# Moving one-time work across a joint, and reordering the queues of the steps behind it

## The reference

```python
x = _layernorm(x + L0(x))   # mixes x scaled by row sums of adj, by their squares, and a softmax's row sums, with one weight
x = _layernorm(x + L1(x))   # A_hat @ x, @ W1.T, batchnorm over all images, relu, @ W2.T, batchnorm
x = _layernorm(x + L2(x))   # two graph convolutions, then LSTMs over windows of 1, 2, 3, 4 nodes
x = _layernorm(x + L3(x))   # h = x @ fc.T + b, then 8 Euler steps:
#   h = h + (1/8) * (sigmoid(alpha)/2 * (adj @ h - h) + h @ w_eff - h + x0),  w_eff = (w * clip(d, 0, 1)) @ w.T
```

## Time and profile before

| | us |
|---|---|
| median of 3 runs | 982.8 (981.35 to 983.01) |
| the profiled execution, its own time | 981.68 |
| its span in the profile | 979.6 |
| TensorE busy | 915.4 (93%) |
| VectorE busy | 645.8 (66%) |
| ScalarE busy | 576.6 (59%) |
| GpSimd busy | 314.6 (32%) |

### The profile page before, as it was taken

The page is one execution under the profiler, slowest core; times in us unless marked ns, Lnnn a source line. Parts: engine busy times, 40 slices in busy tenths (PEclk is TensorE's granted clock), DMA queues, the critical chain, the costliest instruction groups (busy, mean ns, idle before and its releaser), DMA issues.

```text
span 979.6 us, 14819 instructions
## 1 busy us (share of the span) xinstructions
PE 915.4 (93%) x5115; PEld 792.3 (81%) x5115; DVE 645.8 (66%) x1576; ACT 576.6 (59%) x1292; POOL 314.6 (32%) x527
## 2 busy tenths in 40 slices
PE   8799998968899979999999999999999999999996
PEld 6688886346788658998998898899899889978986
DVE  5889995863467755666667666665766666675644
ACT  5467666823464556557737855774685576467352
POOL 2766555411101242035216304421620442150120
PEclk9999999989799989999999999999999999999999
DMA  5321201301011010101100110120011001000100
GB/s 177 119 75 57 74 33 46 122 27 65 0 33 55 1 33 1 54 2 44 56 11 11 33 66 1 44 65 1 12 33 66 1 22 44 1 12 1 33 22 22
DMA packets 26596, 38.56 MB, mean 39 GB/s; under 512 B 3333, under 2 KB 12422, under 8 KB 26010
## 3 DMA queue, kind: packets, MB, share of 16 engines
q1 hardware_dynamic: 26088, 36.05, 11.1%
q10 hardware_dynamic: 434, 1.57, 0.4%
HBM read 21.89 MB, written 15.73 MB: 38 GB/s over the span
## 4 chain that ended last, share of the span: by engine, by line
PE 55%; DVE 9%; POOL 7%; ACT 6%; issue 3%; ACTq 0%; POOLq 0%; DVEq 0%
PE psum L140 16%; PE psum L142 15%; PE psum L141 15%; PE psum L1811 2%; PE psum L1812 2%; PE psum L1815 2%; ACT gate L1378 1%; ACT x L1409 1%; POOL x_rstd L1311 1%; ACT raw L1474 1%; POOL out_rstd L1311 1%; POOL node_l L1329 1%; PE psum L1986 1%; DVE in_h L1543 1%; DVE shared L1617 1%
## 5 line engine op out<-in xcount | busy, mean ns | idle before, releaser
L1378 ACT ACTIVATE gate<-psum,gate_bias 128x256 f32<-128x256 f32 (+2 forms) x296 | 144.1, 559 | 85.2 <-PE psum L1815 62.4
L140 PE MATMUL psum<-in_h,wih_h 128*128 128x256 f32 (+2 forms) x312 | 107.3, 344 | 11.2 <-DVE in_l L1547 7.9
L142 PE MATMUL psum<-in_h,wih_l 128*128 128x256 f32 (+2 forms) x312 | 104.1, 334 | 0.0
L141 PE MATMUL psum<-in_l,wih_h 128*128 128x256 f32 (+2 forms) x312 | 103.6, 332 | 0.0
L1528 DVE TENSOR_TENSOR gate<-gate 128x256 f32<-128x256 f32 (+2 forms) x48 | 23.9, 499 | 88.9 <-ACT gate L1378 88.8
L140 PEld LDWEIGHTS psum<-in_h,wih_h 128*128 128x128 f32 x312 | 59.2, 190 | 22.9 <-DVE in_l L1547 11.6
L1345 POOL TENSOR_TENSOR gate<-in_h,in_l 128x512 f32<-128x512 f32 x14 | 17.9, 1303 | 164.7 <-DVE in_l L1547 164.7
L140 PE MATMUL psum<-e_h,shared 128*128 128x384 f32 x180 | 62.0, 345 | 5.5 <-DVE shared L1617 3.2
L1381 ACT ACTIVATE gate<-cell 128x512 f32<-128x512 f32 (+2 forms) x80 | 40.3, 503 | 42.6 <-DVE cell L1531 35.4
L141 PEld LDWEIGHTS psum<-in_l,wih_h 128*128 128x128 f32 x312 | 59.4, 190 | 5.1 <-issue 0.2
L142 PEld LDWEIGHTS psum<-in_h,wih_l 128*128 128x128 f32 x312 | 59.4, 190 | 4.7
(11 more groups left out here) (398 smaller groups left out, 2940.4 us busy)
## 6 DMA issues: line engine op xcount, KB each, us to landing
x_spill<-x SPq DMA_DIRECT2D x30, 256.0 KB, 2.0
xt<-in_x_t_dram SPq DMA_DIRECT2D x16, 256.0 KB, 2.7
raw<-x_spill SPq DMA_DIRECT2D x16, 256.0 KB, 3.0
o_spill<-xt SPq DMA_DIRECT2D x14, 256.0 KB, 2.0
xt<-o_spill SPq DMA_DIRECT2D x14, 256.0 KB, 3.2
x<-x_spill SPq DMA_DIRECT2D x14, 256.0 KB, 3.4
out_dram<-raw SPq DMA_DIRECT2D x14, 256.0 KB, 2.3
raw<-in_adj_t_dram ACTq DMA_DIRECT2D x1, 1024.0 KB, 8.8
```

The lines of the kernel that those rows point to most:

```text
L140: pe.matmul(dst, lh, rh, start=start, stop=False, **kw)
L141: pe.matmul(dst, lh, rl, start=False, stop=False, **kw)
L142: return pe.matmul(dst, ll, rh, start=False, stop=stop, **kw)
L1378: nc.scalar.activation(gate[q][:, 0:n], banks[GATE_BANK[q]][:, 0:n], ACT.Tanh if q == 2 else ACT.Sigmoid, bias=gate_bias[:, p - 1, q:q + 1 ...
```

## The change

Four edits of order, two functions that move from the first half to the second, and a semaphore wait and a PSUM bank that change. No arithmetic changes.

- Joint: `conv_bias_rows` and `row_sum` leave the loop over images and become pieces of START on VectorE. `columns` goes ahead of `turn_0` there, ScalarE's norms go ahead of the copies of N squared, `weff`'s product goes to a PSUM bank of its own, and the wait for b moves from N squared's tile 0 to `square`.
- Step 0: `turn_0`, `first_3` and `square` share slot 1 on TensorE and VectorE, `twice` goes behind cell 2. On VectorE and GpSimd x3's add and first statistics are issued at the end of step 0, ahead of step 1's first cell (they still wait for TensorE's `hlate`, which stays behind that cell).
- Step 1: x3's norm, split and transpose, and half of the first power, come a slot earlier on all engines; the bias product moves from slot 5 to slot 4.
- FILL (and so steps 2 to 7) on ScalarE: the power copies go ahead of `out_0`, `evens_l` goes from slot 2 to slot 3 behind them.

```diff
@@ -747,30 +747,15 @@
-    def conv_bias_rows():
-        for t in range(NT):
-            nc.vector.tensor_scalar(conv_bias[:, t, :], small["bg0s"][:], row_sums[:, t:t + 1], None, ALU.mult)
...
-    def row_sum():
-        dve.wait_ge(an_ready, 1)
-        nc.vector.memset(vec[:, :, 0], 1.0)
-        chain.link(nc.vector.reduce_sum(vec[:, :, 1], an, AX_X))
-        nc.vector.tensor_tensor(vec[:, :, 1], vec[:, :, 1], rates[:], ALU.mult)
     for b in range(B):
         keep_o2(b, b % 2)
-        if b == 2:
-            dve.wait_ge(c_small, 16 * len(small))
-            conv_bias_rows()
...
-        if b == 12:
-            row_sum()
...
@@ -947,7 +932,7 @@
-    lw, ld, fcw, fcb, bg1s = (small[k] for k in ("lw", "ld", "fcw", "fcb", "bg1s"))
+    lw, ld, fcw, fcb, bg0s, bg1s = (small[k] for k in ("lw", "ld", "fcw", "fcb", "bg0s", "bg1s"))
...
@@ -1129,8 +1114,8 @@
-FILL_ACT = [[], ["x3norm_0", "x3split_0", "evens_h"], ["x3t_0", "norm_0", "evens_l"],
-            ["out_0", "power1_0", "power2_0", "gather0_0"], ["rest_h", "coefs0_0", "prep_1", "weight0_0", "x3norm_1"],
+FILL_ACT = [[], ["x3norm_0", "x3split_0", "evens_h"], ["x3t_0", "norm_0"],
+            ["power1_0", "power2_0", "evens_l", "out_0", "gather0_0"], ["rest_h", "coefs0_0", "prep_1", "weight0_0", "x3norm_1"],
...
@@ -1143,7 +1128,7 @@
-            "coefs1", "inner", "innersum", "innerlow", "hlate", "addlate")
+            "coefs1", "inner", "innersum", "innerlow", "hlate")
...
@@ -1167,34 +1152,35 @@
-START_ACT = ["prep_0", "prep_1", "first_0", "norm_0", "first_1", "norm_1", "gather0_0", "gather0_1", "weight0_0", "weight0_1",
+START_ACT = ["prep_0", "prep_1", "norm_0", "first_0", "norm_1", "first_1", "gather0_0", "gather0_1", "weight0_0", "weight0_1",
...
-START_DVE = ["turn_0", "columns", "turn_1", "weff", "first_0", "first_1", "gather0_0", "gather0_1", "weight0_0", "weight0_1",
+START_DVE = ["columns", "turn_0", "turn_1", "weff", "conv_bias", "first_0", "row_sum", "first_1", "gather0_0", "gather0_1", "weight0_0", "weight0_1",
...
-ONCE_PE = [[], ["square", "twice", "turn_0"], ["first_3"], ["gather0_0", "cube", "second_0"],
+ONCE_PE = [[], ["turn_0", "first_3", "square"], ["twice"], ["gather0_0", "cube", "second_0"],
...
-ONCE_ACT = [["prep_0"], [], ["norm_0", "evens_h", "first_3"], ["evens_l", "gather0_0", "second_0"],
+ONCE_ACT = [["prep_0"], ["first_3"], ["norm_0", "evens_h"], ["evens_l", "gather0_0", "second_0"],
...
-ONCE_DVE = [[], ["square", "twice", "turn_0"], ["first_3"], ["gather0_0", "cube", "second_0"],
+ONCE_DVE = [[], ["turn_0", "first_3", "square"], ["twice"], ["gather0_0", "cube", "second_0"],
...
-            ["gather1_1", "offset", "weight1_1", "input_1"]]
-ONCE_POOL = [[], ["turn_0"], ["norm_0"], [], [], ["turn_1"], ["norm_1"], [], [], [], ["whole"]]
+            ["gather1_1", "offset", "weight1_1", "input_1", "x3add", "x3first"]]
+ONCE_POOL = [[], ["turn_0"], ["norm_0"], [], [], ["turn_1"], ["norm_1"], [], [], [], ["whole", "x3first"]]
...
-NEXT_PE = [["hlate"], ["lift", "turn_0"], ["turn_vec"], ["x3t_0", "power1a_0", "power1b_0", "power2_0", "gather0_0"],
-           ["lift_last", "weight0_0"], ["bias", "coefs0_0", "coefs1_0", "turn_1"]] + FILL_PE[6:]
-NEXT_ACT = [[], ["evens_h"], ["x3norm_0", "x3split_0", "norm_0"], ["x3t_0", "evens_l", "power1_0", "power2_0", "gather0_0"],
-            ["split_e", "rest_h", "prep_1", "weight0_0", "x3norm_1"], ["coefs0_0", "coefs1_0", "x3split_1", "rest_l"]] + FILL_ACT[6:]
-NEXT_DVE = [["addlate"], ["x3sum_0", "lift", "turn_0", "turn_vec"], ["mix_3", "x3sum_1", "mix_4"],
-            ["x3t_0", "power1_0", "power2_0", "gather0_0", "mix_5", "mix_6", "mix_7"],
-            ["lift_last", "weight0_0"], ["bias", "coefs0_0", "coefs1_0", "turn_1"]] + FILL_DVE[6:]
-NEXT_POOL = [[], ["x3sum_0", "turn_0"], ["x3split_0", "norm_0", "x3sum_1"], [], ["split_e"]] + FILL_POOL[5:]
+NEXT_PE = [["hlate"], ["lift", "turn_0"], ["turn_vec", "x3t_0", "power1a_0"], ["power1b_0", "power2_0", "gather0_0"],
+           ["lift_last", "weight0_0", "bias"], ["coefs0_0", "coefs1_0", "turn_1"]] + FILL_PE[6:]
+NEXT_ACT = FILL_ACT[:3] + [["power1_0", "power2_0", "evens_l", "gather0_0"],
+                           ["split_e", "rest_h", "prep_1", "weight0_0", "x3norm_1"],
+                           ["coefs0_0", "coefs1_0", "x3split_1", "rest_l"]] + FILL_ACT[6:]
+NEXT_DVE = [[], ["lift", "turn_0", "turn_vec"], ["x3t_0", "mix_3", "x3sum_1", "mix_4"],
+            ["power1_0", "power2_0", "gather0_0", "mix_5", "mix_6", "mix_7"],
+            ["lift_last", "weight0_0", "bias"], ["coefs0_0", "coefs1_0", "turn_1"]] + FILL_DVE[6:]
+NEXT_POOL = FILL_POOL[:4] + [["split_e"]] + FILL_POOL[5:]
...
@@ -1692,10 +1678,19 @@
+    def conv_bias_rows():
+        for t in range(NT):
+            nc.vector.tensor_scalar(conv_bias[:, t, :], bg0s[:], row_sums[:, t:t + 1], None, ALU.mult)
+    def row_sum():
+        nc.vector.memset(vec[:, :, 0], 1.0)
+        own.link(nc.vector.reduce_sum(vec[:, :, 1], an, AX_X))
+        own.link(nc.vector.tensor_tensor(vec[:, :, 1], vec[:, :, 1], rates[:], ALU.mult))
     def weff():
...
-        nc.vector.scalar_tensor_tensor(out=bp[:, 1, :], in0=tile(UB[0][:], 0), scalar=DT, in1=bp[:, 1, :],
+        nc.vector.scalar_tensor_tensor(out=bp[:, 1, :], in0=tile(banks[0][:], 0), scalar=DT, in1=bp[:, 1, :],
...
@@ -1776,9 +1771,9 @@
-                    "addlate": x3add, "x3low": x3low, "outhalf": out_half,
+                    "x3low": x3low, "outhalf": out_half,
...
-                    "columns": columns, "weff": weff, "bcols": spread_bias, "square": square, "twice": twice, "cube": cube,
+                    "columns": columns, "conv_bias": conv_bias_rows, "row_sum": row_sum, "weff": weff, "bcols": spread_bias, "square": square, "twice": twice, "cube": cube,
...
@@ -1956,13 +1951,11 @@
     def weff():
         pe.wait_ge(lws_ready, 1)
-        pe.matmul(tile(UB[0][:], 0), lws[:], lw[:], start=True, stop=True).then_inc(weff_done, 1)
+        pe.matmul(tile(banks[0][:], 0), lws[:], lw[:], start=True, stop=True).then_inc(weff_done, 1)
...
         if k == 0:
-            if t == 0:
-                pe.wait_ge(b_kept, 1)
...
@@ -1976,6 +1969,7 @@
     def square():
         pe.wait_ge(p_lo, 3)
+        pe.wait_ge(b_kept, 1)
...
```

## The result

The changed kernel takes 950.32 us, median of 4 runs (949.76 to 952.44), against 982.08 (980.14 to 983.01) for the kernel before beside it: ratio 0.9686, 95% interval 0.9666 to 0.9706. The forecast was 951.5 with 946.5 to 962. The profiled execution took 949.76 us, its span 947.8, so the traces differ by 31.8 us in the span.

The account below looks back on a forecast made before the run. TensorE, busy 915.4 of 979.6 us, was taken as the bound, losing time to waits and half clock. Savings 4.5 + 6.9 + 6.7 + 6.0 + 2.0 + 4.9 = 31.0 us gave 950.7, stated as 951.5, range 946.5 to 962.

Parts of the forecast that it names:

- Stage 1: End of the first half: without bias rows and row sums on VectorE, ScalarE sets the pace; 4.5 us saved.
- Stage 2: Start of the second half: the norm's chain bounds the first gather, moved rows cost nothing; 6.9 us saved.
- Stages 3 and 4a: Step 0: twice behind cell 2 at full clock, 6.7 us; step 1: earlier x3 work removes the transpose wait, 6.0 us.
- 4b: Second step: bias product moved ahead of cell 5 removes the 2.4 us wait for L1773; 2.0 us saved.
- 5: Steps 2 to 6: moved power copies and evens_l remove two TensorE waits, 0.97 x 5 = 4.9 us.
- A: Rival: at start, twice and before cell 2 the clock falls longer than allowed, three more stretches; 956.6 us, chance 0.20.
- B: Rival: VectorE's queue carries the moved rows into the first gathers' path, up to 5.5 us; 957 us, chance 0.08.
- C: Rival: in the middle steps another wait replaces the removed ones, 4.9 us given back; 956.4 us, chance 0.10.
- D: Rival: slower than before, TensorE stays at 1.2 GHz through the rebuilt stretch; 985 us, chance 0.02.

Follow-up runs that it names:

- kernel 7: Changed kernel with the bias rows and row sums back in the first half's loop over images (b = 2 and b = 12): 953.03 us, ratio 0.9712.
- kernel 9: Changed kernel with the row sums computed three times in their new place: 955.73 us, ratio 0.9755.
- kernel 8: Changed kernel with the bias rows alone back in the loop over images, at b = 10: 949.57 us, ratio 0.9682.
- kernel 3: Kernel before with the new lists of steps 0 and 1 alone, FILL as before: 971.07 us, ratio 0.9888.
- kernel 5: Changed kernel with evens_l back in slot 2 of the middle steps, powers still ahead of out_0: 954.17 us, ratio 0.9725.
- Kernel 4: Changed kernel with the Euler bias back in slot 5 on both engines: 951.75 us, ratio 0.9697.
- kernel 10: Changed kernel with x3's add and first statistics back behind step 1's first cells: 952.46 us, ratio 0.9713.
- kernel 12: Changed kernel with idle 512-column TensorE passes in four waits (step 0, step 1, two in the last LSTM step): 945.34 us, ratio 0.9643.
- Kernel 2: Kernel before with the new ScalarE order of the middle steps alone: 973.98 us, ratio 0.9925.
- kernel 6: Changed kernel with evens_l and out_0 ahead of the powers in slot 3 of the middle steps: 959.99 us, ratio 0.9790.

## Why the forecast came out

**Right, with its own steps.** Stage 1: ScalarE's pace sets the loop once both rows are out. 4.95 against 4.5, of which 0.6 was there before the loop began; kernel 7 shows 2.8 of it as VectorE's and 1.6 as the clock's. Stage 2: the norm's chain is the new bound, 9.2 us behind ScalarE's first instruction against 9.1 by the chain alone (I had taken 9.5 to allow for a fall of the clock, which did not come). The moved rows were priced at nothing for a cover of about 1.5 us; kernel 9 measured 1.6. The bias rows took 0.28 each and 0.87 together, under the 1.1 of four times's shortest, since they start 0.20 apart; no 512-wide work of GpSimd fell on them. The rule weighed there (the Trainium skill, GPSIMD Engine Reference, Specifications: SBUF interfaces shared with VectorE, with contention for VectorE's instructions in a 2-port mode or with two SBUF inputs) fits kernels 7 and 8, though no view here names the mode of the bias rows: 3.04 us for four beside the last three of GpSimd's four scalings (L397) and 1.67 beside part of one instruction of its 128x512 size; beside GpSimd's 128x4 root of 1.01 us the trace shows none of it. Stages 3 and 4a: 7.4 and 6.0 against 6.7 and 6.0, with one half-clock stretch each in the changed kernel's trace, as allowed (kernels 3 and 5 had two in step 0); the wait before cell 2 is the 2.66 forecast as 2.8.

**Mis-sized, 4b.** "removes the 2.4 wait for L1773: 2.0." The wait named was the last of several things behind cell 5's update on VectorE. With it gone, the low parts of the first coefficients, which stand behind the same update, are late next (1.58); 0.44 was added in front, and the clock fell at 346 for some 1.5. I priced the removed wait and didn't ask, as elsewhere, what is late next. Kernel 4 shows the edit's own worth as nothing within the measurement. Where the clock did not fall at 346 (kernels 10 and 12) the stage takes 26.04 us against 26.39 before, so 0.35 of the forecast 2.0 came and the clock took the rest and more; what 4a had pulled forward met the same VectorE work in any case.

**Mis-sized, 5.** "Both waits go: 0.97 x 5 = 4.9; ends 0 to 5.3." The mechanism was right, waits and step count too. The size was taken from idle brackets and bounded by the stretch's unfilled 1.06 us, and both undercount: a pass of 0.23 us pitch is drawn 0.39 long, so each wait swallows what is drawn past the pitch, and the first pass behind it is drawn longer. TensorE of the kernel before, around the two brackets of the earlier trace rows:

```profile
454.43 0.39 PE L142 MATMUL psum<-adj_h,node_l 128*128 128x512 f32 x1
...
455.41 0.32 PE L141 MATMUL psum<-in_l,wih_h 128*128 128x340 f32 x1
...
456.50 0.32 PE L142 MATMUL psum<-in_h,wih_l 128*128 128x340 f32 x1
...
457.74 0.34 PE L141 MATMUL psum<-e_l,shared 128*128 128x384 f32 x1
```

From start to start, less the pitch (0.23, and 0.16 for the narrower passes), the two waits are 0.49 and 0.79; the pass behind each starts another 0.10 late. That makes 1.5 us. Kernel 2 shows 1.44 a step for this edit alone, the changed kernel 1.53 (steps 83.56 apart, where 84.1 was forecast). My upper bound of 5.3 was therefore no bound: 7.6 came.

**Rivals.** A (three more stretches than allowed) did not come: ahead of the closing one four are left, 13.6 us in all, where five held 34.1. B would have begun from 1.6 us of extra work on VectorE. Its "some 1.5 us of slack even at full price" was too kind: VectorE idles 0.59 us behind the bias rows, so by my estimate at 3.04 us in place of 0.87 they would have used the 0.59 and the whole 1.6. C is what kernels 5 and 6 build on purpose: 0.7 and 2.0 us a step. D's point was never near, the longest stretch seen in any run being 13.65 us.

**The sum.** Part of the closeness is luck: 4b and 5 miss by 3.2 and 2.7 us in opposite ways. The last step of the sum has a slip as well: 950.7 and 1.1 make 951.8, not 951.5.

**Open.** Why the clock falls in one execution and not in another behind the same wait (180, 320, 346, 848) is not settled, and the stretch near 38 was not looked into; it moves single terms by 1.4 to 1.6 us, and the stages above rest on one trace of each kernel.

## What to carry to other kernels

Price a wait of a pipelined engine from the start of one instruction to the start of the next, less the pitch, not from the idle time shown, and take a "busy" of 98.8% as no upper bound on the gain. Before a difference of one or two us between two traces is put down to an edit, compare their half-clock stretches. When an instruction is moved ahead of a wait, look for the second one that stands behind the same producer. An instruction that waits for a slow engine, such as a normalization behind a root, belongs behind everything in its queue that TensorE will want.

## What the runs showed of the hardware

- Behind the same 1.94 to 1.95 us wait of TensorE at about 179.4, the granted clock fell to 0.50 for 3.41 us in the kernel before and in kernel 3, and stayed at 1.00 in kernels 2 and 7: 19.50 or 17.93 us for the same 40 passes.
- With idle passes in a 2.66 and a 2.12 us wait the clock was at 1.00 behind them (kernel 12) where it had been 0.50, 1.4 us each; without them it also stayed at 1.00 behind 2.64 and 2.11 us in kernel 8. Over all executions the mean granted clock was 0.992 to 0.996 with them and 0.985 to 0.991 in the changed kernel.
- At or right behind 32 one-column passes (3.73 us at full clock) the clock fell with and without 1.04 us of idle time before them, for 3.41 us in most traces and 6.83 in those of kernels 3, 5 and 8; in that of kernel 9 it did not fall.
- Four 128x128 multiplications on VectorE took 0.87 us alone, 1.67 with part of one 128x512 two-operand instruction of GpSimd beside them, and 3.04 with such instructions throughout. Beside GpSimd's 128x4 root of 1.01 us they kept their 0.28 each.
